# Split prefetch of the p window in the down projection of a Mamba layer with a ternary FFN

## The chip, the cores and the metric

The kernel runs on 8 cores of one Trainium2 chip, one batch row per core. The metric is device time in microseconds of the slowest core, lower is better.

## The reference, cut to what matters

The layer adds a Mamba block and a ternary gated FFN to its input. The part touched by the change is the last matrix product of the FFN, `ternary_matmul(p, W_d)`:

```python
def ternary_matmul(x, w):
    return jnp.matmul(x, jnp.sign(w).T)
xq = activation_quant(rms_norm(x))
g = jax.nn.silu(ternary_matmul(xq, W_g))
u = ternary_matmul(xq, W_u)
p = g * u
return ternary_matmul(p, W_d)
...
xn = _layernorm(x, axis=-1)
x = x + mamba(xn, ...) + ffn(xn, W_g, W_u, W_d)
```

Per core, x is 2048 tokens by 2048 features, p is 2048 tokens by 8192, and `W_d` is 2048 by 8192. So the product is [2048 x 8192] by [8192 x 2048], with weights that are only +1, 0 or -1.

## The kernel before, in words

The program records instructions by hand into one stream for each engine (`streams`), in the order of the Python code. `W` adds a wait on an engine's own counter (`ve`, `sc`, `te`, `gp`), `I` adds an instruction, `LD` adds a load issued by SyncE on a lane (a semaphore `la0` to `la16`), `ST` adds a store issued by GpSimd (`sa0` to `sa7`), and `WT` waits for a load or a store. An engine works its stream strictly in order. All large tiles are views into one SBUF tensor `PA`, so almost every row of the profile names `PA`; the line number tells them apart.

The stages in order of time:

1. Statistics, quantisation and transposes (lines 210 to 334).
2. The input projection, with the casts of the gate and up weights beside it (lines 336 to 439). Its matmuls are line 414.
3. Eight chunks of 256 tokens: convolution, selective scan and output gate on VectorE and ScalarE, with the gate and up products of the FFN on TensorE in between (lines 441 to 742). p goes to the DRAM tensor `psp`, laid out [128, 4 windows, 64, 512].
4. The down projection (lines 744 to 810), the stage that the change touches.
5. The output projection of the Mamba block, and the final sum (lines 812 to 885). Its matmuls are line 862; its window loads (line 851, `ygsp`) are 4 MB each.

Stage 4 runs over `mg` (4 groups of 512 output features). For each group it loads sixteen 1 MB pieces of `wdT` through two staging slots (line 768, lanes 10 and 11), and ScalarE writes their signs as bf16 into `wdb` (line 776), a single buffer of 64 blocks of 512 columns. The load of a piece waits until the Sign two pieces earlier has freed its slot; the first Sign of a group waits for the last matmul of the group before. Then `wdw` runs over 4 windows of 512 tokens. For each, SyncE waits for the last matmul of the window before (`te_p6a_grp`), and loads the whole 8 MB window of p into the single buffer `pwin` (line 786, lane 12). Then `ms` runs over 4 blocks of 128 output features: 64 matmuls of 128x512 accumulate in one PSUM bank (line 794), ScalarE copies the bank to `ostf` (line 801, two slots), and GpSimd stores it to `offn` (line 805). Banks `pb0` to `pb3` rotate as `(ms + wdw) % 4`.

```python
W("sync", "te", te_p6a_grp)
t_pw = LD(lambda e, w=wdw: e.dma_start(
    out=pwin[:], in_=psp[:, w, :, :]), 12)
for ms in range(4):
    bank = (ms + wdw) % 4
    ...
    WT("tensor", t_pw)
    W("tensor", "sc", ev_bank6[bank])
    for k in range(KH):
        I("tensor", ... wdb[:, k, ms * 128:(ms + 1) * 128], pwin[:, k, :] ...)
te_p6a_grp = C["te"]
```

In SyncE's stream the four window loads of a group stand behind the sixteen `wdT` loads of that group, and the `wdT` loads of the next group behind them.

Of the kernel before, what the change touches and what calls it, by code (L numbers as in the profile page):

```python
# [24 lines left out]
KH = H // 128  # L25
# [7 lines left out]
def build_program():  # L33
# [23 lines left out]
    psp = nc.dram_tensor("psp", [128, 4, KH, 512], BF16, kind="Internal").ap()  # L57
# [3 lines left out]
    C = {"ve": 0, "sc": 0, "te": 0, "gp": 0}  # L61
# [5 lines left out]
    with contextlib.ExitStack() as ctx:  # L67
# [4 lines left out]
        def W(eng, sem, val):  # L72
            if val and val > 0:
                streams[eng].append(lambda e, s=sems[sem], v=val: e.wait_ge(s, v))
# [3 lines left out]
        def I(eng, builder, sem=None, amt=1, nodep=False):  # L78
            own = _SELF.get(eng)
            if nodep:  # L80
                own = None
            if own is not None and C[own] > 0 and sem is not None:
                streams[eng].append(
                    lambda e, s=sems[own], v=C[own]: e.wait_ge(s, v))
            if sem is not None:
                C[sem] += amt
                streams[eng].append(
                    lambda e, b=builder, s=sems[sem], a=amt: b(e).then_inc(s, a))
            else:
                streams[eng].append(lambda e, b=builder: b(e))  # L90
            return C[sem] if sem else None

        def LD(builder, lane):
            i = lane
            ld_cnt[i] += 16
            streams["sync"].append(
                lambda e, b=builder, s=ldsem[i]: b(e).then_inc(s, 16))
            return ("L", i, ld_cnt[i])
# [15 lines left out]
        def WT(eng, *toks):  # L114
            for tok in toks:
                if tok is None:
                    continue
                kind, i, v = tok
                s = ldsem[i] if kind == "L" else stsem[i]
                streams[eng].append(lambda e, s=s, v=v: e.wait_ge(s, v))  # L120

        def st_snap():
# [24 lines left out]
        pb = [ctx.enter_context(nc.psum_tensor(f"pb{i}", [128, 512], F32))  # L147
              for i in range(8)]
# [12 lines left out]
        def vb(off_f32, *shape):  # L161
            n = int(np.prod(shape))
            ap = PAb[:, 2 * off_f32: 2 * off_f32 + n]
            if len(shape) == 3:
                ap = ap.rearrange("p (a b c) -> p a b c", b=shape[1], c=shape[2])
            elif len(shape) == 2:
                ap = ap.rearrange("p (a b) -> p a b", b=shape[-1])
            return ap
# [111 lines left out]
        for tt in range(NT):  # L280
# [47 lines left out]
            for h2 in range(2):  # L328
                t_qtt = ST(lambda e, tt=tt, h2=h2: e.dma_start(
                    out=qsp[:, h2 * 8:(h2 + 1) * 8, tt * 128:(tt + 1) * 128],  # L330
                    in_=qtt[:, h2 * 8:(h2 + 1) * 8, :]), 0)
# [59 lines left out]
        for mg in range(16):  # L391
# [14 lines left out]
            for ms in range(4):  # L406
                row = mg * 4 + ms
                xsl = ms % 2
                for wdw in range(4):
                    bank = (ms * 4 + wdw) % 4  # L410
                    W("tensor", "ve", ev_cast)
                    W("tensor", "ve", ev_bank_sc[bank])
                    for k in range(16):
# [3 lines left out]
                            start=(k == 0), stop=(k == 15)), "te")  # L417
# [11 lines left out]
                    out=dst[:, drow, :], in_=xzst[:, xsl, :]), 1 + xsl)  # L429
# [109 lines left out]
        for cI in range(NCH):  # L539
# [6 lines left out]
            if cI == 0:  # L546
# [3 lines left out]
                out=qwin[:, h2 * 8:(h2 + 1) * 8, :],  # L550
                in_=qsp[:, h2 * 8:(h2 + 1) * 8, col0:col0 + TCH]), 7)
# [3 lines left out]
            if cI == 0:  # L555
# [10 lines left out]
                for q4 in range(4):  # L566
                    t_xpre = LD(lambda e, q4=q4: e.dma_start(
                        out=xpre[:, q4 * 8:(q4 + 1) * 8, 3:259],
                        in_=xsp[:, q4 * 8:(q4 + 1) * 8, 0:TCH]), 5)
            else:  # L570
                for q4 in range(4):
                    t_xpre = LD(lambda e, col0=col0, q4=q4: e.dma_start(
                        out=xpre[:, q4 * 8:(q4 + 1) * 8, :],
                        in_=xsp[:, q4 * 8:(q4 + 1) * 8, col0 - 3: col0 + TCH]), 5)
            W("sync", "ve", ev_zread_ve)
            for q4 in range(4):
                t_z = LD(lambda e, col0=col0, q4=q4: e.dma_start(
                    out=zb[:, q4 * 8:(q4 + 1) * 8, :],
# [107 lines left out]
            for dt in range(KDI):  # L686
# [27 lines left out]
                if g == 7:  # L714
# [5 lines left out]
                        in_=yg8[:]), 5)  # L720
# [26 lines left out]
        MARKS["P5"] = {k: len(v) for k, v in streams.items()}  # L747

        wdb = vb(0, KH, 512)
        pwin = vb(16384, KH, 512)  # L750
        wd_big = [vf(32768, 4, 512), vf(34816, 4, 512)]
        wdT_t = wdT.rearrange("(k p) l -> p k l", p=128)
        ostf = vf(36864, 2, 512)
        t_ost2 = [None, None]
        te_p6a_grp = 0
        ev_bank6 = [sc_p3] * 4
        ev_sgn = [0, 0]
        W("tensor", "ve", ve_p3)
        for mg in range(4):
            for q in range(16):  # L760
                sl = q % 2
                if mg == 0 and q == 0:
                    W("sync", "ve", ve_p5)
                    W("sync", "sc", sc_p5)
                    for tok in snap_p3:
                        WT("sync", tok)
                W("sync", "sc", ev_sgn[sl])
                t_wd = LD(lambda e, q=q, mg=mg, sl=sl: e.dma_start(
                    out=wd_big[sl][:],
                    in_=wdT_t[:, q * 4:(q + 1) * 4, mg * 512:(mg + 1) * 512]), 10 + sl)  # L770
                WT("scalar", t_wd)
                if mg == 0 and q == 0:
                    W("scalar", "ve", ve_p5)
                if q == 0:
                    W("scalar", "te", te_p6a_grp)
                ev_sgn[sl] = I("scalar", lambda e, q=q, sl=sl: e.activation(
                    wdb[:, q * 4:(q + 1) * 4, :].rearrange("p a b -> p (a b)"),
                    wd_big[sl][:].rearrange("p a b -> p (a b)"), AF.Sign), "sc")
            sc_wd = C["sc"]
            for wdw in range(4):  # L780
                if mg == 0 and wdw == 0:
                    for tok in snap_p5:
                        WT("sync", tok)
                    W("sync", "ve", ve_p5)
                W("sync", "te", te_p6a_grp)
                t_pw = LD(lambda e, w=wdw: e.dma_start(
                    out=pwin[:], in_=psp[:, w, :, :]), 12)
                for ms in range(4):
                    bank = (ms + wdw) % 4
                    W("tensor", "sc", sc_wd)  # L790
                    WT("tensor", t_pw)
                    W("tensor", "sc", ev_bank6[bank])
                    for k in range(KH):
                        I("tensor", lambda e, k=k, ms=ms, bank=bank: e.matmul(  # L794
                            pb[bank][:], wdb[:, k, ms * 128:(ms + 1) * 128], pwin[:, k, :],
                            start=(k == 0), stop=(k == KH - 1)), "te")
                    te_mm = C["te"]
                    W("scalar", "te", te_mm)
                    osl = (ms + 4 * wdw) % 2
                    WT("scalar", t_ost2[osl])  # L800
                    sc_ost = I("scalar", lambda e, bank=bank, osl=osl: e.activation(
                        ostf[:, osl, :], pb[bank][:], AF.Copy), "sc")
                    ev_bank6[bank] = sc_ost
                    W("gpsimd", "sc", sc_ost)
                    t_ost2[osl] = ST(lambda e, mg=mg, ms=ms, w=wdw, osl=osl: e.dma_start(
                        out=offn[:, mg * 4 + ms, w * 512:(w + 1) * 512], in_=ostf[:, osl, :]), 1 + 3 * osl)
                te_p6a_grp = C["te"]
        snap_p6a = st_snap()
        sc_p6a = C["sc"]
# [161 lines left out]
```

## Time and profile before

| what | us |
|---|---|
| median of 2 runs | 13253.68 (13243.57 to 13263.78) |
| the profiled execution, its own time | 13226.75 |
| its span, slowest core (core 3) | 13225.2 |
| spans of the eight cores | 13171.5 to 13225.2 |
| stage 4, first load of `wdT` to the last matmul, core 3 | 10868.5 to 12405.2 |

Times in the profile are counted from the first instruction of the core. "PE" is TensorE's matmuls and "PEld" its weight loads, "DVE" is VectorE, "ACT" ScalarE, "POOL" GpSimd and "SPq" the loads issued by SyncE. Matmul records overlap each other (each lasts longer than the distance to the next), so the rate of matmuls is read from a run of them, not from the mean of one. PEclk is the clock that TensorE was granted, as a share of its full speed of 2.4 GHz.

### The profile page before, as it was taken

What the parts mean: (1) busy time and instruction counts of PE and PEld (TensorE: products, weight loads), DVE (VectorE), ACT (ScalarE), POOL (GpSimd) and SP (SyncE); (2) the same over time, 40 slices, a digit from 0 to 9 for tenths busy, and PEclk for the clock granted to TensorE, in tenths of its full rate; (3) what the DMA queues carried; (4) which work ended last, traced back from release to release, by engine and by line L of the source; (5) the groups of instructions that cost most, each with busy time, mean ns of one, the idle gap of its engine ahead of it and who ended that gap; (6) DMA issues with size and microseconds to landing.
All of it is one profiled execution on the core that took longest, in us unless ns stands there. A gap on an engine that the chain in (4) does not pass through costs nothing.

```text
span 13225.2 us, 104989 instructions; the slowest of 8 cores (13171.5 to 13225.2 us)
## 1 busy us (share of the span) xinstructions
PE 5051.7 (38%) x28160; PEld 3051.0 (23%) x28160; DVE 7270.3 (55%) x8002; ACT 4306.0 (33%) x7239; POOL 767.6 (6%) x1286
## 2 busy tenths in 40 slices
PE   0116666333223323323313322323323326556666
PEld 0002222122222212212212212212212222222222
DVE  7661111368768768858858858867886870000011
ACT  1221222254344444434434434434435440111000
POOL 0002222100000000000000000000000000000000
PEclk9999888666666656656656666666666668778778
DMA  2106676412212212212212211222221233333354
GB/s 85 33 23 191 194 208 205 143 62 89 88 47 91 91 44 91 90 48 89 89 52 83 91 65 70 91 66 70 89 81 62 84 104 138 148 147 138 147 196 172
DMA packets 607800, 1354.33 MB, mean 102 GB/s; under 512 B 43504, under 2 KB 387696, under 8 KB 533232
## 3 DMA queue, kind: packets, MB, share of 16 engines
q1 hardware_dynamic: 539632, 1154.60, 26.5%
q0 software_dynamic: 67584, 193.02, 4.0%
q8 instruction: 236, 3.87, 0.1%
q14 instruction: 348, 2.85, 0.1%
HBM read 1154.51 MB, written 192.94 MB: 102 GB/s over the span
## 4 chain that ended last, share of the span: by engine, by line
DVE 44%; DMA 18%; PE 13%; ACT 12%; issue 11%; SPq 1%; DVEq 1%; ACTq 0%; POOL 0%; POOLq 0%
DVE PA L692 13%; DVE PA L696 9%; PE pb L794 7%; ACT dA L680 5%; DMA wgusp<-PA 5%; DVE PA L673 4%; PE pb L862 4%; DMA PA<-wuT 3%; DMA PA<-psp 3%; DVE PA L697 2%; DVE PA L300 2%; DMA PA<-ygsp 2%; DVE PA L588 2%; DVE PA L592 2%; DMA PA<-wgT 2%
## 5 line engine op out<-in xcount | busy, mean ns | idle before, releaser
L503 PE MATMUL pb<-PA 128*128 128x256 bf16 x8192 | 1377.3, 340 | 4480.9 <-DVE PA L529 4464.3
L692 DVE TENSOR_TENSOR_SCAN PA<-dA,hcar,PA 128x256 f32<-128x256 f32 x3840 | 2494.6, 726 | 39.3 <-ACT dA L680 14.6
L680 ACT ACTIVATE dA<-PA,a_sb 128x256 f32<-128x256 bf16 x3840 | 1949.4, 508 | 477.0 <-DVE PA L673 134.8
L503 PEld LDWEIGHTS pb<-PA 128*128 128x128 bf16 x8192 | 966.7, 120 | 4812.7 <-issue 4547.0
L877 DVE TENSOR_TENSOR PA<-pb,PA 128x512 f32<-128x512 f32 x64 | 44.3, 692 | 2255.1 <-PE pb L862 2255.1
L680 ACT ACT_TABLE_LOAD x240 | 307.9, 1283 | 2702.3 <-DVE PA L673 2702.3
L794 PE MATMUL pb<-PA 128*128 128x512 bf16 x4096 | 929.1, 391 | 633.9 <-DMA PA<-psp 633.9
L414 PE MATMUL pb<-PA 128*128 128x512 bf16 x4096 | 958.3, 398 | 499.7 <-DVE PA L398 379.4
L696 DVE TENSOR_TENSOR PA<-PA 128x4096 bf16<-128x4096 f32 x256 | 1133.0, 4426 | 27.7 <-DVE PA L692 1.4
L507 PE MATMUL pb<-PA 128*128 128x256 bf16 x8192 | 1098.1, 293 | 0.0
L507 PEld LDWEIGHTS pb<-PA 128*128 128x128 bf16 x8192 | 874.4, 107 | 170.3
L422 DVE CAST PA<-pb 128x512 bf16<-128x512 f32 x256 | 177.1, 692 | 1183.8 <-DMA xsp<-PA 467.3
L363 ACT ACTIVATE PA<-PA 128x512 bf16<-128x512 f32 x512 | 322.2, 629 | 1184.9 <-DMA PA<-wuT 621.0
L536 POOL DMA_DIRECT2D psp<-PA x512 | 276.1, 539 | 7433.1 <-DVE PA L529 7396.0
L794 PEld LDWEIGHTS pb<-PA 128*128 128x128 bf16 x4096 | 409.8, 100 | 1153.0 <-issue 710.0
L414 PEld LDWEIGHTS pb<-PA 128*128 128x128 bf16 x4096 | 413.5, 102 | 1044.2 <-issue 610.9
L529 DVE TENSOR_TENSOR PA<-PA,pb 128x256 bf16<-128x256 bf16 x512 | 215.7, 421 | 784.7 <-DMA psp<-PA 679.2
L862 PE MATMUL pb<-PA 128*128 128x512 bf16 x2048 | 506.4, 415 | 302.9 <-DMA PA<-ygsp 302.9
L673 DVE TENSOR_TENSOR PA<-PA 128x4096 bf16<-128x4096 bf16 x256 | 586.7, 2292 | 27.0 <-DVE PA L671 0.5
L665 DVE TENSOR_TENSOR PA<-PA 128x2048 bf16<-128x2048 bf16 x32 | 73.4, 2293 | 752.7 <-ACT PA L663 752.7
L613 PE MATMUL pb<-PA,wx_bf 128*128 128x256 bf16 x256 | 47.3, 371 | 1100.6 <-DVE PA L607 1100.6
L314 PE MATMUL pb<-identb,PA 128*128 128x128 bf16 x512 | 127.7, 265 | 886.6 <-DVE PA L303 860.6
(101 smaller groups left out, 5314.0 us busy)
## 6 DMA issues: line engine op xcount, KB each, us to landing
PA<-wgusp SPq DMA_DIRECT2D x512, 1024.0 KB, 4.7
PA<-winT SPq DMA_DIRECT2D x32, 2048.0 KB, 21.0
PA<-wgT SPq DMA_DIRECT2D x256, 256.0 KB, 4.3
wgusp<-PA POOLq DMA_DIRECT2D x512, 128.0 KB, 3.9
PA<-wuT SPq DMA_DIRECT2D x256, 256.0 KB, 4.2
PA<-wdT SPq DMA_DIRECT2D x64, 1024.0 KB, 6.2
PA<-ygsp SPq DMA_DIRECT2D x16, 4096.0 KB, 14.0
PA<-xrow SPq DMA_DIRECT2D x32, 1024.0 KB, 4.8
```

What stands on the lines that cost most here:

```text
L300: I("vector", lambda e, c=cbit: e.scalar_tensor_tensor(tq, mk, -c, tq, ALU.mult, ALU.add), "ve")
L363: csc[sl] = I("scalar", lambda e, sl=sl: e.activation(cslot_b[sl][:], cslot_f[sl][:].rearrange("p a b -> p (a b)"), AF.Sign), "sc")
L414: I("tensor", lambda e, k=k, ms=ms, w=wdw, bank=bank: e.matmul(pb[bank][:], wbf[:, k, ms * 128:(ms + 1) * 128], xnT[:, k, w * 512:(w + 1) ...
L503: I("tensor", lambda e, k=k, bank=bank, sl=sl: e.matmul(bank[:, 0:TCH], wgu_sl[sl][:, 0, k, :], qwin[:, k, :], start=(k == 0), stop=(k == ...
L507: I("tensor", lambda e, k=k, bank=bank, sl=sl: e.matmul(bank[:, TCH:2 * TCH], wgu_sl[sl][:, 1, k, :], qwin[:, k, :], start=(k == 0), stop= ...
L536: sl2=sl2: e.dma_start(out=psp[:, w4, ht, coff:coff + TCH], in_=pst2[:]), 6 + sl2)
L673: return I("vector", lambda e: e.tensor_tensor(dbx_b[:], dxdtb[:].unsqueeze(1).broadcast_to([128, DS, TCH]), b_all[:], ALU.mult), "ve")
L680: exp_sc[n] = I("scalar", lambda e, dt=dt, n=n: e.activation(dAs_t[n][:], delta[:, dt, :], AF.Exp, scale=a_sb[:, dt, n:n + 1]), "sc")
L692: I("vector", lambda e, n=n, dt=dt: e.tensor_tensor_scan(hall[:, n, :], dAs_t[n][:], dbx_b[:, n, :], hcar[:, dt, n:n + 1], ALU.mult, ALU.a ...
L696: I("vector", lambda e: e.tensor_tensor(ct[:], hall[:], c_all[:], ALU.mult), "ve")
L794: I("tensor", lambda e, k=k, ms=ms, bank=bank: e.matmul(pb[bank][:], wdb[:, k, ms * 128:(ms + 1) * 128], pwin[:, k, :], start=(k == 0), st ...
L862: I("tensor", lambda e, k=k, ms=ms, bank=bank: e.matmul(pb[bank][:], wob[:, k, ms * 128:(ms + 1) * 128], ygwin[:, k, :], start=(k == 0), s ...
```

## The change

`pwin` is cut into two halves, `pwinH[0]` (k 0 to 31) and `pwinH[1]` (k 32 to 63), each with a lane of its own (12 and 13) and in the same place of `PA` as before. Each window is now worked in two passes: k 0 to 31 for all four `ms`, which opens four banks, then k 32 to 63 for all four, which closes them one by one; only then are they copied out. The first half's buffer is loaded with the next window as soon as the first pass has ended, the second half's as soon as the second has. The two halves of the very first window are loaded ahead of the stage's first `wdT` piece. The window after the last of a group is window 0 again, so the prefetch runs on across groups.

```diff
-        pwin = vb(16384, KH, 512)
+        pwinH = [vb(16384, 32, 512), vb(24576, 32, 512)]
...
+        W("sync", "te", te_p3c)
+        for tok in snap_p3:
+            WT("sync", tok)
+        pw_tok = [LD(lambda e, h=h: e.dma_start(
+            out=pwinH[h][:], in_=psp[:, 0, h * 32:(h + 1) * 32, :]), 12 + h)
+            for h in range(2)]
...
-                W("sync", "te", te_p6a_grp)
-                t_pw = LD(lambda e, w=wdw: e.dma_start(
-                    out=pwin[:], in_=psp[:, w, :, :]), 12)
+                widx = mg * 4 + wdw
+                nw = (widx + 1) % 4
+                W("tensor", "sc", sc_wd)
+                WT("tensor", pw_tok[0])
                 for ms in range(4):
                     bank = (ms + wdw) % 4
-                    W("tensor", "sc", sc_wd)
-                    WT("tensor", t_pw)
                     W("tensor", "sc", ev_bank6[bank])
-                    for k in range(KH):
+                    for k in range(32):
                         I("tensor", lambda e, k=k, ms=ms, bank=bank: e.matmul(
-                            pb[bank][:], wdb[:, k, ms * 128:(ms + 1) * 128], pwin[:, k, :],
-                            start=(k == 0), stop=(k == KH - 1)), "te")
+                            pb[bank][:], wdb[:, k, ms * 128:(ms + 1) * 128],
+                            pwinH[0][:, k, :],
+                            start=(k == 0), stop=False), "te")
+                pw_te[0] = C["te"]
+                if widx + 1 < 16:
+                    W("sync", "te", pw_te[0])
+                    pw_tok[0] = LD(lambda e, nw=nw: e.dma_start(
+                        out=pwinH[0][:], in_=psp[:, nw, 0:32, :]), 12)
+                WT("tensor", pw_tok[1])
+                for ms in range(4):
+                    bank = (ms + wdw) % 4
+                    for k in range(32):
+                        I("tensor", lambda e, k=k, ms=ms, bank=bank: e.matmul(
+                            pb[bank][:], wdb[:, 32 + k, ms * 128:(ms + 1) * 128],
+                            pwinH[1][:, k, :],
+                            start=False, stop=(k == 31)), "te")
                     te_mm = C["te"]
...
+                pw_te[1] = C["te"]
+                if widx + 1 < 16:
+                    W("sync", "te", pw_te[1])
+                    pw_tok[1] = LD(lambda e, nw=nw: e.dma_start(
+                        out=pwinH[1][:], in_=psp[:, nw, 32:64, :]), 13)
                 te_p6a_grp = C["te"]
```

SyncE's stream before, from the start of stage 4 into its second group (`te`, `sc`, `ve` are the engines' counters, `sa0` to `sa7` the stores):

```order
L768 DMA PA<-wdT 128x4x512 [waits ve,sc,sa0,sa1,sa2,sa3,sa4,sa5,sa6,sa7]
L768 DMA PA<-wdT 128x4x512
L768 DMA PA<-wdT 128x4x512 [waits sc] x14
L786 DMA PA<-psp 128x32768 [waits sa0,sa1,sa2,sa3,sa4,sa5,sa6,sa7,ve]
L786 DMA PA<-psp 128x32768 [waits te] x3
L768 DMA PA<-wdT 128x4x512 [waits sc] x16
L786 DMA PA<-psp 128x32768 [waits te] x4
```

SyncE's stream of the changed kernel, from the start of stage 4:

```order
L765 DMA PA<-psp 128x16384 [waits ve,sc,te,sa0,sa1,sa2,sa3,sa4,sa5,sa6,sa7]
L765 DMA PA<-psp 128x16384
L778 DMA PA<-wdT 128x4x512 [waits ve,sc,sa0,sa1,sa2,sa3,sa4,sa5,sa6,sa7]
L778 DMA PA<-wdT 128x4x512
L778 DMA PA<-wdT 128x4x512 [waits sc] x14
L806 DMA PA<-psp 128x16384 [waits te]
L829 DMA PA<-psp 128x16384 [waits te]
```

The window's two halves moved from behind the sixteen pieces to ahead of them. The same stream of the changed kernel, where the first group ends and the second begins:

```order
L806 DMA PA<-psp 128x16384 [waits te]
L829 DMA PA<-psp 128x16384 [waits te]
L778 DMA PA<-wdT 128x4x512 [waits sc] x16
L806 DMA PA<-psp 128x16384 [waits te]
L829 DMA PA<-psp 128x16384 [waits te]
```

Before, nothing that waits for TensorE's last matmul of the group stood ahead of the next group's `wdT` pieces; now the load of line 829 does, and they are issued behind it.

TensorE's stream before, at the end of the first window and the start of the second (`pb` is the bank, `la12` the lane of the window load):

```order
L794 MATMUL pb3<-PA 128x512 [waits sc,la12]
L794 MATMUL pb3<-PA 128x512 x63
L794 MATMUL pb1<-PA 128x512 [waits sc,la12]
L794 MATMUL pb1<-PA 128x512 x63
L794 MATMUL pb2<-PA 128x512 [waits sc,la12]
L794 MATMUL pb2<-PA 128x512 x63
```

The same place in the changed kernel, from the last bank of the first pass of window 1 to the first pass of window 2:

```order
L799 MATMUL pb3<-PA 128x512 [waits sc]
L799 MATMUL pb3<-PA 128x512 x31
L812 MATMUL pb0<-PA 128x512 [waits la13]
L812 MATMUL pb0<-PA 128x512 x31
L812 MATMUL pb1<-PA 128x512 x32
L812 MATMUL pb2<-PA 128x512 x32
L812 MATMUL pb3<-PA 128x512 x32
L799 MATMUL pb1<-PA 128x512 [waits sc,la12]
L799 MATMUL pb1<-PA 128x512 x31
L799 MATMUL pb2<-PA 128x512 [waits sc]
L799 MATMUL pb2<-PA 128x512 x31
```

A bank is now opened once, left, and closed 128 matmuls later, and the four banks are closed at a distance of 32 matmuls instead of 64.

## Rows read from the trace of the kernel before

**Rows 1.** Part 5 of the page: the matmuls of stage 4.

```profile
L794 PE MATMUL pb<-PA 128*128 128x512 bf16 x4096 | 929.1, 391 | 633.9 <-DMA PA<-psp 633.9
```

**Rows 2.** Timeline of TensorE in stage 4 (start, us, what, [idle before <-releaser]), 8 of 16 windows.

```profile
10955.31 57.90 PE L794 MATMUL pb<-PA 128*128 128x512 bf16 x256 [113.14 <-DMA PA<-psp]
11036.57 58.22 PE L794 MATMUL pb<-PA 128*128 128x512 bf16 x256 [23.36 <-DMA PA<-psp]
...
11200.90 57.98 PE L794 MATMUL pb<-PA 128*128 128x512 bf16 x256 [24.20 <-DMA PA<-psp]
11340.33 58.23 PE L794 MATMUL pb<-PA 128*128 128x512 bf16 x256 [81.46 <-DMA PA<-psp]
11421.42 56.96 PE L794 MATMUL pb<-PA 128*128 128x512 bf16 x256 [22.85 <-DMA PA<-psp]
...
11720.76 57.47 PE L794 MATMUL pb<-PA 128*128 128x512 bf16 x256 [81.86 <-DMA PA<-psp]
...
12100.24 57.17 PE L794 MATMUL pb<-PA 128*128 128x512 bf16 x256 [80.15 <-DMA PA<-psp]
...
12341.00 64.21 PE L794 MATMUL pb<-PA 128*128 128x512 bf16 x256 [22.81 <-DMA PA<-psp]
```

**Rows 3.** Timeline of TensorE in stage 2: one run of 64 matmuls.

```profile
1522.77 13.97 PE L414 MATMUL pb<-PA 128*128 128x512 bf16 x64 [1.89 <-DVE PA L422]
```

**Rows 4.** Timeline, SyncE's loads and the outer Signs, first and second group.

```profile
10868.53 61.70 SPq L768 DMA_DIRECT2D PA<-wdT  x16
10874.88 1.91 ACT L776 ACTIVATE PA<-PA 128x2048 bf16<-128x2048 f32 x1 [14.15 <-DMA PA<-wdT]
...
10935.86 1.91 ACT L776 ACTIVATE PA<-PA 128x2048 bf16<-128x2048 f32 x1 [1.62 <-DMA PA<-wdT]
...
11177.18 138.71 SPq L768 DMA_DIRECT2D PA<-wdT  x16
...
11259.77 3.91 ACT L776 ACTIVATE PA<-PA 128x2048 bf16<-128x2048 f32 x2
...
11315.99 82.99 SPq L786 DMA_DIRECT2D PA<-psp  x2
11320.88 1.91 ACT L776 ACTIVATE PA<-PA 128x2048 bf16<-128x2048 f32 x1 [2.81 <-DMA PA<-wdT]
```

**Rows 5.** Chain of waits: window loads of 8 MB (`psp`) and of 4 MB (`ygsp`).

```profile
11398.64 22.53 DMA PA<-psp
...
12528.49 13.90 DMA PA<-ygsp
...
12681.93 12.96 DMA PA<-ygsp
...
12831.40 18.84 DMA PA<-ygsp
```

**Rows 6.** DMA issues: KB each, median us from issue to landing.

```profile
PA<-wdT SPq DMA_DIRECT2D x64, 1024.0 KB, 6.2
PA<-ygsp SPq DMA_DIRECT2D x16, 4096.0 KB, 14.0
```

**Rows 7.** The stores of line 805, by line.

```profile
DMA to landing us min/median/max: 2.3/2.3/17.8
```

**Rows 8.** Windows, core 3: busy (x) of PE PEld DVE ACT POOL, PEclk, DMA share, GB/s.

```profile
11440.00:11460.00 20.00, 20.00 (x94) 9.11 (x93) 0.00 (x0) 0.60 (x1) 0.54 (x1) 1.00 0.04 15
...
12380.00:12400.00 20.00, 20.00 (x78) 8.27 (x76) 0.00 (x0) 0.60 (x1) 0.54 (x1) 0.81 0.04 14
11640.00:11720.00 80.00, 0.00 (x0) 0.00 (x0) 0.00 (x0) 30.34 (x16) 0.54 (x1) 0.52 0.84 292
11398.00:11421.00 23.00, 0.57 (x3) 0.07 (x1) 0.00 (x0) 0.60 (x1) 0.54 (x1) 0.56 0.90 376
...
1780.00:1800.00 20.00, 20.00 (x94) 9.07 (x93) 2.77 (x4) 5.04 (x8) 5.33 (x10) 1.00 0.73 208
```

**Rows 9.** Windows in stage 5, core 2, then core 0: same columns.

```profile
12411.00:12440.00 29.00, 28.60 (x104) 11.73 (x105) 4.16 (x6) 0.00 (x0) 1.62 (x3) 0.77 0.20 56
...
12420.00:12440.00 20.00, 20.00 (x91) 8.93 (x90) 2.77 (x4) 0.00 (x0) 1.08 (x2) 0.97 0.30 72
```

More of the change, by code:

```diff
@@ L755, in build_program @@
         te_p6a_grp = 0
+        te_p3c = C["te"]
         ev_bank6 = [sc_p3] * 4
@@ L758, in build_program @@
         W("tensor", "ve", ve_p3)
+        W("sync", "ve", ve_p5)
+        W("sync", "sc", sc_p5)
+        W("sync", "te", te_p3c)
[4 more added lines that the diff above has]
+            for h in range(2)]
+        pw_te = [0, 0]
         for mg in range(4):
@@ L780, in build_program @@
             for wdw in range(4):
[L781 to L784, printed above, removed]
-                W("sync", "te", te_p6a_grp)
-                t_pw = LD(lambda e, w=wdw: e.dma_start(
-                    out=pwin[:], in_=psp[:, w, :, :]), 12)
+                widx = mg * 4 + wdw
+                nw = (widx + 1) % 4
+                W("tensor", "sc", sc_wd)
+                WT("tensor", pw_tok[0])
                 for ms in range(4):
                     bank = (ms + wdw) % 4
-                    W("tensor", "sc", sc_wd)
-                    WT("tensor", t_pw)
                     W("tensor", "sc", ev_bank6[bank])
-                    for k in range(KH):
+                    for k in range(32):
                         I("tensor", lambda e, k=k, ms=ms, bank=bank: e.matmul(
-                            pb[bank][:], wdb[:, k, ms * 128:(ms + 1) * 128], pwin[:, k, :],
-                            start=(k == 0), stop=(k == KH - 1)), "te")
+                            pb[bank][:], wdb[:, k, ms * 128:(ms + 1) * 128],
[14 more added lines that the diff above has]
+                            start=False, stop=(k == 31)), "te")
                     te_mm = C["te"]
```

## The prediction

> **What bounds the kernel now.** I read the page's groups first. The matmuls of the down projection (line 794) are busy for 929.1 us, and ahead of them TensorE sat idle for 633.9 us, all of it until a load of `psp` landed [rows 1]. The timeline of TensorE shows how these are spread: sixteen windows of 256 matmuls, some 57 to 58 us each. Ahead of the first window of a group the gap is 113.14, 81.46, 81.86 and 80.15 us; ahead of the twelve others it is about 23 us [rows 2]. The twelve sum to 633.9 - (113.14 + 81.46 + 81.86 + 80.15) = 277.3 us. The reader is to see strict alternation: the load of an 8 MB window takes 22.53 us in the chain of waits [rows 5], TensorE does nothing meanwhile, and while TensorE computes, the DMA engines stand at a share of 0.04 [rows 8]. Nothing else in this stage ends last: the bank copies and the stores run beside the matmuls. The long gaps have another content: sixteen Signs of `wdT` pieces and then the window load [rows 4].
>
> **The twelve inner gaps.** After the change a half window (4 MB) is loaded while the other half is computed. How long is a pass of 128 matmuls? From a run of 64 in 13.97 us [rows 3], of which one record is about 0.38 us, the distance is (13.97 - 0.38) / 63 = 0.2157 us; a pass is 27.6 us and a window 256 x 0.2157 + 0.2 = 55.4 us. How long is a 4 MB load? `ygsp` windows have that size: 12.96 and 13.90 us where they run alone, 18.84 at the longest where they share [rows 5], 14.0 in the median [rows 6]. So 13 us lie under 27.6 us, and even 19 would. The gaps go: 277.3 us.
>
> **The clock's start.** In a gap the granted clock falls to 0.52 or 0.56, near the lower of its two levels (1.2 of 2.4 GHz), and within a window it is 1.00 [rows 8]. So each window starts slow. The sixteen windows took 929.1 us [rows 1] where sixteen at full clock take 16 x 55.4 = 886.4. Of the 42.7 us over, 6.3 belong to the last window, which took 64.21 instead of some 57.9 [rows 2]. That leaves 36.4 / 16 = 2.3 us a window. Twelve windows will follow without a gap: 12 x 2.3 = 27 us.
>
> **The three later group starts.** Before, the first two `wdT` pieces of a group were issued 82 us before its first Sign (11177.18), the first Sign ran at 11259.77, the sixteenth at 11320.88, and the window load was issued at 11315.99 [rows 4]; the gap was 81.46 us [rows 2]. Now SyncE must first wait for the group's last matmul and issue the second half of the window, and the pieces stand behind it. One half takes 13 us, and a 1 MB piece behind it comes about 2.8 us later (8 MB in 22.53 us [rows 5]). So the first Sign starts some 16 us after the last matmul. The pace afterwards stays: 61.1 us from the first to the sixteenth Sign (11320.88 - 11259.77; 60.98 in the first group [rows 4]) and 1.9 for the last one. Both halves are in SBUF by then, so matmuls start at 16 + 61.1 + 1.9 = 79 us. Gain: 2 to 2.5 us each, 7 together. It is small because what the half window saves at the end it costs at the start: the prefetch of the pieces is given up.
>
> **The stage's start.** Before: 10868.53 (first issue) to 10955.31 (first matmul), 86.8 us [rows 2, 4]. Now 22.5 us for both halves, about 2.8 for the first piece, then 61 and 1.9: 88.2, plus a little issue time, so 2 us lost. With the line above it makes +5. The bounds of the two: if pieces and half share the engines without delay, the group starts gain up to 13 us each (the half simply vanishes), +39; if the pieces come as late as with the 18.84 us load [rows 5], -6 us each, -18. I take +5, since a load of 4 MB takes 13 to 14 us in two of the three rows and in the median.
>
> **Waits that the change adds.** The halves' waits stand ahead of a pass, on TensorE; behind them is the whole stage, and they are met as worked out above. The four banks are now closed 6.9 us apart instead of 13.8. ScalarE's copy waits for the store of two copies earlier, which is 13.8 us back; stores land in 2.3 us, at the longest in 17.8 [rows 7]. One store of 17.8 us would hold a copy by some 4 us, and TensorE wants a closed bank again no earlier than 14 us after its closing (the bank order in front of the next window is turned by one). So I cost it at 0; with the cover gone it would be 4 us a window. The matmuls' number and size do not change. Sync's other loads are not in this stage.
>
> **Sum.** 277.3 + 27 + 7 - 2 = 309 us. The profiled execution took 13226.75, so it becomes 12918. It stands 26.9 under the median of the runs, 13253.68, which becomes 12945. That is 2.3% less. A measurement of this kernel can tell about 2% from no change, 265 us, which leaves 44 us of room, so the size of what is given back decides how it counts.
>
> **Rival 1: the denser work brings a lower clock.** In core 3's last window the rate fell from 94 matmuls in 20 us at a clock of 1.00 to 78 at 0.81 [rows 8], and in stage 5 core 2 stood at 0.77 while core 0 stood at 0.97 in the same microseconds [rows 9]. So there is a state at about 0.81, which came while TensorE was busy on all cores. After the change TensorE has runs of 4 x 55.4 = 221 us instead of 58. At 0.81 a window costs 55.4 / 0.81 - 55.4 = 13.0 us more. If all sixteen are so, 208 less the 6.3 already paid: 202 given back, and the time is 12945 + 202 = 13147. With eight windows, 98 given back: 13043. From 44 / 13.0 = 3.4 windows more than now, the result is within 2%. Against it: fifteen of core 3's sixteen windows took 57 to 58 us, with all eight cores in this stage at the same time, so 58 us of dense matmuls do not bring it. For it: no row shows a run longer than that, and the slowest core counts, of eight. The Trainium skill ("TensorE: Matmul & The Clock Gate", Part 1: The HAM clock gate) warns that once three cores of a die run dense matmuls a current limiter takes the whole die to 13/16 of the full clock and holds it there; it adds that this depends on the data. The level agrees with the 0.81 of the rows, the reach does not: here single cores are slowed and most windows never are. Taken literally the rule would have each window already at 13/16, which they are not, and the change would then give nothing back; as a risk that grows with density it is this rival.
>
> **Rival 2: the prefetch is only half covered.** If the eight cores, whose loads now overlap matmuls, crowd each other or the stores, a half may take longer than its pass. Each us beyond 27.6 costs 24 us over the 24 inner halves. The 44 us of room are gone at 29.4 us for a half, and at 32 us the time is 12945 + 106 = 13051. For it: 18.84 us where a 4 MB load shared the engines [rows 5]. Against: the eight cores already load 8 MB in 22.5 us at 376 GB/s at nearly the same time [rows 8], and the mean need falls to 4 MB in 27.6 us, 152 GB/s.
>
> **Rival 3, the slower side: DMA writes into SBUF slow the matmuls.** Before, matmuls of this stage ran with the DMA engines at 0.04 [rows 8]; now a load lies beside half of their time, and writes the same tensor that TensorE reads. The place is the 24 inner passes, 665 us. It decides for slower than before only if these passes take 309 / 665 = 46% longer, 40 us each instead of 27.6; at 60% longer the time is 12945 + 399 = 13344. Against: in stage 2, 94 matmuls ran in 20 us at a DMA share of 0.73 and 208 GB/s [rows 8], the same rate as without any.
>
> **Chances.** The forecast 60%, the lower clock in enough windows to matter 32%, the half covered prefetch 5%, the slower matmuls 3%. The range begins at 12895 (the last window's 6 us and up to 39 at the group starts gained) and must leave out no more than 2 in 10: it ends at 13110, between eight windows at the lower clock (13043) and all sixteen (13147). Faster by over 2% (under 12989) holds in the forecast and a little of rival 1: 0.62. Within 2%: 0.35. Slower by over 2%: 0.03.
>
> **What would show it.** TensorE's timeline in the down projection should show four runs of about 224 us without a gap, then gaps of some 79 us; idle ahead of these matmuls waiting for `psp` should be under 10 us in the inner windows. A first Sign 16 us after a group's last matmul, and a half landing in 13 to 19 us, are the other two steps. The granted clock within a run should be 1.00; a clock near 0.81, or under 90 matmuls in 20 us, is rival 1. Gaps between passes are rival 2. A full clock with under 90 matmuls in 20 us is rival 3. The forecast is wrong if core spans fall by less than 265 us.

## The result, and the profile after

The changed kernel took 12969.84 us in the median of 11 runs (12897.29 to 13157.75); the kernel before took 13256.27 us (10 runs) beside it. The ratio is 0.9767, with a 95% interval of 0.9725 to 0.981. Run again later on another chip the ratio was 0.9723 (0.9635 to 0.9811). Both ratios are taken over the executions in which no die lagged behind at a lower clock (9 of these 11, later 2 of 6), so the first isn't the quotient of the medians, which is 0.9784. The forecast was 12945 us, a ratio of 0.9767 to the 13253.68 us known then: faster, by a little more than the 2% that a measurement can tell. That the kernel got faster is clear; that it did so by more than 2% is likely and not settled, since both intervals reach a little over 0.98. That forecast and measurement agree to the fourth digit is luck.

The page of the changed kernel shows the matmuls of the down projection, in two groups for the two passes, and the groups view shows their idle time:

```profile
L799 PE MATMUL pb<-PA 128*128 128x512 bf16 x2007 | 451.6, 385 | 345.8 <-ACT PA L786 343.6 <-issue 0.2
L812 PE MATMUL pb<-PA 128*128 128x512 bf16 x2007 | 442.3, 379 | 2.2
```

They answer to [rows 1]. No idle time is put down to a load of `psp` any more; what is left is four waits for the last Sign (line 786), 343.6 us in all. (Some 2% of the matmul records are missing from this trace, hence 2007 of 2048.)

Timeline of TensorE, changed kernel, core 2, the first group, then the first pass of the other three; the columns are those of [rows 2]:

```profile
10997.08 30.18 PE L799 MATMUL pb<-PA 128*128 128x512 bf16 x125 [116.04 <-ACT PA L786]
11027.09 27.79 PE L812 MATMUL pb<-PA 128*128 128x512 bf16 x125
11054.72 27.79 PE L799 MATMUL pb<-PA 128*128 128x512 bf16 x126
11082.34 27.79 PE L812 MATMUL pb<-PA 128*128 128x512 bf16 x125
...
11192.85 27.79 PE L812 MATMUL pb<-PA 128*128 128x512 bf16 x125
11297.28 30.45 PE L799 MATMUL pb<-PA 128*128 128x512 bf16 x125 [76.65 <-ACT PA L786]
...
11596.24 1.01 PE L799 MATMUL pb<-PA 128*128 128x512 bf16 x2 [75.12 <-ACT PA L786]
...
11894.85 30.33 PE L799 MATMUL pb<-PA 128*128 128x512 bf16 x126 [75.76 <-ACT PA L786]
...
12090.78 27.79 PE L812 MATMUL pb<-PA 128*128 128x512 bf16 x126
```

The reader is to see eight passes that follow each other every 27.63 us with nothing in between, then one long gap. Only the first pass of a group is longer, by 2.4 to 2.7 us: that is the slow start of the clock, which each of the sixteen windows paid before. Two windows of the view, with the columns of [rows 8], show the clock and the DMA in a gap and in a run:

```profile
11240.00:11290.00 50.00, 0.00 (x0) 0.00 (x0) 0.00 (x0) 24.95 (x14) 0.00 (x0) 0.50 0.83 271
11360.00:11380.00 20.00, 19.95 (x93) 9.04 (x93) 0.00 (x0) 0.00 (x0) 0.00 (x0) 1.00 0.35 145
```

In the gap the clock stands at 0.50, the lower of its levels (1.2 GHz), in the run at 1.00 (2.4 GHz). The loads of the first half, by line, landed in:

```profile
DMA to landing us min/median/max: 12.5/13.3/14.9
```

The loads of the second half (line 829) take 12.8 to 14.5 us. One half takes half of the pass that covers it.

### The profile page after: what moved, and what is told of

Same layout as the page of the kernel before. It is cut to its first block, busy times and chain, and to the rows that moved or that the text cites. A ratio compares the mean times of both kernels' runs of the same rounds, so it can differ in the third digit from the quotient of the medians.

```text
span 12919.3 us, 104737 instructions; the slowest of 8 cores (12870.3 to 12919.3 us)
## 1 busy us (share of the span) xinstructions
PE 4983.0 (39%) x27955; PEld 3029.2 (23%) x28160; DVE 7270.3 (56%) x8002; ACT 4305.9 (33%) x7239; POOL 760.1 (6%) x1286
## 4 chain that ended last, share of the span: by engine, by line
DVE 46%; DMA 16%; PE 13%; issue 12%; ACT 12%; SPq 1%; DVEq 1%; ACTq 0%; POOL 0%; POOLq 0%
DVE PA L692 14%; DVE PA L696 9%; ACT dA L680 5%; DMA wgusp<-PA 5%; DVE PA L673 5%; DMA PA<-wuT 3%; PE pb L799 3%; PE pb L812 3%; PE pb L886 3%; DVE PA L697 2%; DVE PA L300 2%; DMA PA<-ygsp 2%; DMA PA<-wdT 2%; DVE PA L588 2%; DVE PA L592 2%
## 5 line engine op out<-in xcount | busy, mean ns | idle before, releaser
L503 PEld LDWEIGHTS pb<-PA 128*128 128x128 bf16 x8192 | 958.7, 119 | 4821.8 <-issue 4551.4
L414 PE MATMUL pb<-PA 128*128 128x512 bf16 x4014 | 968.9, 403 | 529.1 <-DVE PA L398 401.3
L507 PEld LDWEIGHTS pb<-PA 128*128 128x128 bf16 x8192 | 871.2, 106 | 172.2
L414 PEld LDWEIGHTS pb<-PA 128*128 128x128 bf16 x4096 | 417.6, 103 | 1080.2 <-issue 655.8
L886 PE MATMUL pb<-PA 128*128 128x512 bf16 x2007 | 472.9, 397 | 317.2 <-DMA PA<-ygsp 314.6
L799 PE MATMUL pb<-PA 128*128 128x512 bf16 x2007 | 451.6, 385 | 345.8 <-ACT PA L786 343.6
L812 PE MATMUL pb<-PA 128*128 128x512 bf16 x2007 | 442.3, 379 | 2.2
```

The lines of the kernel that those rows point to most:

```text
L414: I("tensor", lambda e, k=k, ms=ms, w=wdw, bank=bank: e.matmul(pb[bank][:], wbf[:, k, ms * 128:(ms + 1) * 128], xnT[:, k, w * 512:(w + 1) ...
L503: I("tensor", lambda e, k=k, bank=bank, sl=sl: e.matmul(bank[:, 0:TCH], wgu_sl[sl][:, 0, k, :], qwin[:, k, :], start=(k == 0), stop=(k == ...
L507: I("tensor", lambda e, k=k, bank=bank, sl=sl: e.matmul(bank[:, TCH:2 * TCH], wgu_sl[sl][:, 1, k, :], qwin[:, k, :], start=(k == 0), stop= ...
L799: I("tensor", lambda e, k=k, ms=ms, bank=bank: e.matmul(pb[bank][:], wdb[:, k, ms * 128:(ms + 1) * 128], pwinH[0][:, k, :], start=(k == 0) ...
L812: I("tensor", lambda e, k=k, ms=ms, bank=bank: e.matmul(pb[bank][:], wdb[:, 32 + k, ms * 128:(ms + 1) * 128], pwinH[1][:, k, :], start=Fal ...
L886: I("tensor", lambda e, k=k, ms=ms, bank=bank: e.matmul(pb[bank][:], wob[:, k, ms * 128:(ms + 1) * 128], ygwin[:, k, :], start=(k == 0), s ...
```

## The experiments

Six of the eight runs change one thing in the changed kernel or build on it; two repeat kernels. To set the kernels side by side without the cores that were granted a lower clock (more on them below), "undisturbed span" here means the median span of those cores, over all executions, whose mean granted clock was within 0.003 of the highest of that kernel. It is 13189.5 us for the kernel before (122 of 248 core spans) and 12882.9 us for the changed one (86 of 144): 307 us less. e1 to e4 ran on one chip, e5 and e6 on a second, e7 and e8 on a third; the kernel before, run beside them, had an undisturbed span of 13197, 13170 and 13194 us there, so a comparison across chips can be off by some 25 us.

**e1: no overlap.**

```diff
-                if widx + 1 < 16:
-                    W("sync", "te", pw_te[0])
-                    pw_tok[0] = LD(... pwinH[0] ...)
...
                     W("sync", "te", pw_te[1])
+                    pw_tok[0] = LD(... pwinH[0] ...)
                     pw_tok[1] = LD(... pwinH[1] ...)
```

> The changed kernel with one edit: the first half's next load is no longer issued after the first pass but, like the second half's, after the window's last matmul. Two passes, two halves and the bank order stay. Theory (the gain is the load time that now lies under matmuls): each of the 12 inner gaps comes back as the time of one 4 MB load, 13 to 14 us, plus 2.3 us of slow clock, about 190 us; the second half lands under the first pass. At the three group starts a second 4 MB load stands ahead of the wdT pieces, 9 us each, 28 us. Together +218 us over the changed kernel, near 0.995 of the kernel before. Rival (the two-pass order of the banks, not the overlap, brought the gain): stays within 20 us of the changed kernel.

Measured: 13221.32 us, ratio to the kernel before 0.9949 (0.9918 to 0.998), undisturbed span 13098 us, 215 over the changed kernel where 218 were expected. Timeline of TensorE, core 4:

```profile
11054.19 30.64 PE L799 MATMUL pb<-PA 128*128 128x512 bf16 x128 [13.33 <-DMA PA<-psp]
11084.66 27.79 PE L808 MATMUL pb<-PA 128*128 128x512 bf16 x128
11125.68 30.73 PE L799 MATMUL pb<-PA 128*128 128x512 bf16 x128 [13.23 <-DMA PA<-psp]
11156.25 27.79 PE L808 MATMUL pb<-PA 128*128 128x512 bf16 x128
11272.58 30.67 PE L799 MATMUL pb<-PA 128*128 128x512 bf16 x128 [88.54 <-ACT PA L786]
```

The gap is back, with the slow start behind it, and it is 13.3 us rather than 23, because the second half lands under the first pass. Splitting the load brings 10 us a window, and issuing it a pass earlier the rest. The order of the banks brings nothing by itself: e1 is 92 us under the kernel before, and twelve gaps that are 10 us shorter, less three group gaps that are some 8 us longer (86.82 to 90.06 us), leave nothing for it.

**e2: each half loaded twice.**

```diff
                     pw_tok[0] = LD(... pwinH[0] ...)
+                    if wdw < 3:
+                        WT("sync", pw_tok[0])
+                        pw_tok[0] = LD(... pwinH[0] ...)
```

and the same for the second half.

> The changed kernel, but within a group each half is loaded, awaited, and loaded a second time, so that twice the bytes lie beside the inner passes: two loads of 13 us are 26 us, under a pass of 27.6 us. Theory (a half is covered with a factor of two to spare, and DMA writes beside the matmuls do not slow them): within 20 us of the changed kernel, matmuls at 0.2157 us, inner gaps under 1 us. Rival 2 of the prediction (crowding makes a half take longer than its pass when traffic is higher): gaps of several us in each of 21 inner passes, +50 us or more. Rival 3 (DMA writes into SBUF slow the matmuls): passes longer than 27.8 us at a full clock.

Measured: 13034.85 us, ratio 0.9801 (0.9728 to 0.9875), undisturbed span 12942 us, 59 over the changed kernel. That is a miss for my "within 20 us", and on the side of rival 2, for which I had written 50 us or more. Timeline of TensorE and the landing of line 806's loads, core 2:

```profile
11089.56 30.04 PE L799 MATMUL pb<-PA 128*128 128x512 bf16 x128 [6.31 <-DMA PA<-psp]
11119.43 27.79 PE L816 MATMUL pb<-PA 128*128 128x512 bf16 x128
11149.99 27.79 PE L799 MATMUL pb<-PA 128*128 128x512 bf16 x128 [2.77 <-DMA PA<-psp]
11178.75 27.79 PE L816 MATMUL pb<-PA 128*128 128x512 bf16 x128 [0.97 <-DMA PA<-psp]
...
DMA to landing us min/median/max: 13.3/14.9/16.7
```

With twice the bytes (DMA share 0.79 from 10993 to 11217 us, 278 GB/s) a load of the first half takes 14.9 us instead of 13.3, and its repetition 15.4; for the second half it is 16.2 and 14.5 instead of 14.0. Two take 30.3 or 30.7 us, over the 27.6 us of a pass; the inner gaps sum to 45 us, and several restart at a slow clock (29.2 to 30.0 us a pass). Crowding (rival 2) is real, but at most some 2 us a load in size: the cover has a factor of 1.8, not endless. Rival 3 is refuted: passes that follow without a long gap last 27.79 us with twice the DMA writes beside them, to the hundredth what they last in the changed kernel.

**e3: the second half behind the pieces.**

```diff
             sc_wd = C["sc"]
+            if mg > 0:
+                W("sync", "te", pw_te[1])
+                pw_tok[1] = LD(... pwinH[1], psp[:, 0, 32:64, :] ...)
...
-                if widx + 1 < 16:
+                if widx + 1 < 16 and wdw < 3:
                     W("sync", "te", pw_te[1])
```

> The changed kernel with one load moved: at the three group changes the second half of the window is issued behind the sixteen wdT pieces instead of ahead of them, so that the first two pieces are prefetched again. Theory (the group's start is the first piece's wait for that half plus the chain of Signs): the first Sign follows the last matmul by under 1 us instead of 16, the group gaps fall from 75 to 77 us to 64 us (0.7 + 61.1 + 1.9), and the second half, issued some 56 us after the last matmul, lands before the second pass wants it. 3 x 12 = 36 us less than the changed kernel. Rival (the pace of pieces is set by DMA throughput and the half only moves): no gain, or a new wait ahead of the second pass.

Measured: 12994.74 us, ratio 0.9759 (0.9666 to 0.9851), undisturbed span 12847 us, 36 under the changed kernel where 36 were expected; the ratios themselves are too close to tell the two apart, so the gain is read from the timeline. Timeline around a group change, core 0:

```profile
11169.66 0.60 ACT L824 ACTIVATE PA<-pb 128x512 f32<-128x512 f32 x1 [6.31 <-PE pb L816]
11170.35 3.91 ACT L786 ACTIVATE PA<-PA 128x2048 bf16<-128x2048 f32 x2
...
11223.76 0.46 SPq L792 DMA_DIRECT2D PA<-psp  x1
...
11230.91 4.40 PE L803 MATMUL pb<-PA 128*128 128x512 bf16 x13 [61.45 <-ACT PA L786]
```

The first Sign follows the last bank copy at once, the gap is 61.45 us, and the half issued at 11223.76 is not waited for: the pass behind it starts at 11259.97 without idle time. The other two group gaps of this core are 60.77 and 61.65 us.

**e4: Signs early.** The sixteen pieces of a group are no longer worked in a block. On ScalarE two Signs of the next group stand ahead of each bank copy of the last window's second pass, and eight behind them; TensorE's first pass waits for the eighth Sign, its second for the sixteenth.

```diff
+                if last and nxt:
+                    W("scalar", "te", pw_te[0])
                 for ms in range(4):
+                    if last and nxt:
+                        step(mg + 1, 2 * ms)
+                        step(mg + 1, 2 * ms + 1)
...
+                if last and nxt:
+                    W("scalar", "te", pw_te[1])
+                    for q in range(8, 16):
+                        step(mg + 1, q)
```

(`step` is one Sign and the load of a later piece; the loads of the two halves stand behind the loads of pieces 5 and 9.)

> A version that may beat both: the Signs of the next group's first eight pieces run beside the second pass of the last window (their half of the weights is no longer read then), the other eight beside the first pass of the next group; the window's halves are issued among the pieces, and the stage starts likewise with a first pass after eight pieces. Theory (the group gap is a chain of sixteen Signs at 3.9 to 4.1 us each that nothing but the single weight buffer forbids to hide): the gap ahead of a group falls to about 8 us, another of about 12 us stands ahead of its second pass, so 3 x 56 = 168 us less than the changed kernel, and some 25 us at the stage's start: near 12780 us. Rival (the chip is out of DMA throughput there: 12 MB in a pass of 27.6 us is over 400 GB/s, above the 376 GB/s seen): the gaps add up to 40 us or more a group, and the gain is under 110 us.

Measured: 12901.45 us, ratio 0.9674 (0.9582 to 0.9766), undisturbed span 12723 us, 160 under the changed kernel where some 190 were expected, and the median is 121 us over the 12780 of the expectation; 24 of the 32 core spans were at the lower clock. Timeline of TensorE at a group change, core 2:

```profile
11140.89 27.79 PE L836 MATMUL pb<-PA 128*128 128x512 bf16 x128
11180.70 30.32 PE L823 MATMUL pb<-PA 128*128 128x512 bf16 x128 [12.02 <-ACT PA L782]
11226.45 29.63 PE L836 MATMUL pb<-PA 128*128 128x512 bf16 x128 [15.44 <-ACT PA L782]
```

The 76 us have become 12 and 15: 27 to 30 us at the three group changes instead of the 20 expected, below the 40 of the rival.

**e5: a third staging slot.**

```diff
-        wd_big = [vf(32768, 4, 512), vf(34816, 4, 512)]
+        wd_big = [vf(32768, 4, 512), vf(34816, 4, 512), vf(37888, 4, 512)]
```

> The early-Signs version with a third staging slot for wdT pieces. In it the gaps ahead of a group were 10 to 13 us and ahead of its second pass 15 to 17 us, all until a Sign. Theory A (the gaps are the ping-pong of two slots: a piece's 6 us to land plus its Sign, twice): with three slots the eight pieces come faster, both gaps fall by half or more, 3 x 14 = 42 us and some 15 us at the start less than with two. Theory B (DMA throughput: pieces and halves, 12 MB in a pass, already take all that the engines give): less than 15 us change in all.

Measured: 12831.79 us, ratio 0.9662 (0.9555 to 0.977), undisturbed span 12667 us, 55 under e4, but on another chip, where the kernel before was 27 us shorter too. Core 1 of this trace beside core 2 of e4's, both undisturbed in this stage, shows 37 (start of the stage 10, three group changes 27), between the 57 of theory A and the 15 of theory B. Its timeline and its windows:

```profile
11138.28 30.22 PE L823 MATMUL pb<-PA 128*128 128x512 bf16 x128 [9.23 <-ACT PA L782]
11177.67 29.31 PE L836 MATMUL pb<-PA 128*128 128x512 bf16 x128 [9.18 <-ACT PA L782]
```

```profile
11118.00:11146.00 28.00, 18.77 (x77) 7.88 (x75) 0.00 (x0) 10.79 (x8) 1.08 (x2) 0.82 0.99 363
```

Between the two theories: the ping-pong was part of it. Around the start of the group the DMA engines are now at 0.99 and 363 GB/s, where e4 had 0.92 and 321 GB/s in the same 28 us (11160 to 11188 on its core 2). That throughput is what is left is likely; no run shows it.

**e6: the output projection too.** `ygwin` becomes two buffers of 4 MB, and the load of window i + 1 is issued at the head of window i.

```diff
-        ygwin = vb(8192, KDI, 512)
+        ygwin2 = [vb(8192, KDI, 512), vb(28672, KDI, 512)]
...
+                for yn in ([0, 1] if yi == 0 else [yi + 1]):
+                    if yn < 16:
+                        W("sync", "te", yg_te[yn % 2])
+                        yg_tok[yn % 2] = LD(... ygwin2[yn % 2], ygsp[:, yn % 4, :, :] ...)
```

> The version with three slots, and the output projection's window of ygsp (4 MB) double-buffered in free SBUF, each load issued one window ahead. The same mechanism in the next stage: 12 inner gaps of 13 to 14 us (some 17) plus 2.3 us of slow clock each, 190 us, and the window load at each group start, 13 to 17 us, about 50 us. Together 230 us less than the three-slot version if a matmul stage gains what its uncovered loads took. Rival (in this stage TensorE waits next for the final sum on VectorE or for the xcol and offn loads, which share the DMA engines): under 120 us, with waits for VectorE ahead of the matmuls.

Measured: 12690.14 us, ratio 0.9556 (0.9456 to 0.9657), undisturbed span 12493 us, 174 under e5 (same chip) where 230 were expected. Timeline of TensorE in that stage, core 5:

```profile
11897.59 112.91 PE L926 MATMUL pb<-PA 128*128 128x512 bf16 x512 [39.54 <-DMA PA<-ygsp]
12043.37 113.40 PE L926 MATMUL pb<-PA 128*128 128x512 bf16 x512 [32.86 <-ACT PA L902]
```

The twelve inner gaps are gone (512 matmuls in one run). The gaps at the group changes are not: 32.86, 33.74 and 37.36 us against 35.13, 32.02 and 31.80 in e5. In e5 (core 1) the window load had been the last to land, at 12097.80, and the fourth cast of a `woT` piece (there line 900) had ended 8.7 us earlier. So in that gap at most 9 us could be gained, not the 13 to 17 I had counted. In e6 the gap ends with the fourth cast (line 902), and the casts themselves come later: the first `woT` piece is issued 4.4 us ahead of the group's last matmul (12006.14 against 12010.50) where it was 11.0 us in e5, and its cast starts 8.5 us behind that matmul where it was 2.0. On cores 0 and 1, both at the lower clock in e6, these gaps did fall, from 31.7 to 35.1 us in e5 to 24.4 to 25.8. That is most of the 50 us I had counted too much. Why the pieces are issued later was not tested.

**e7 and e8: the lower clock.** The changed kernel and the kernel of e6, unchanged, in more runs beside the kernel before.

> The changed kernel as it is, beside the kernel before on the same chip, to count cores at the lower clock (mean granted clock more than 0.006 below the highest of the kernel). Rival 1 (denser matmuls bring the lower clock): a clearly larger share of such cores than in the kernel before, and a slowest core that lies further above the undisturbed cores. Theory (the lower clock comes to pairs of cores in either kernel and is not the change's): shares alike within the scatter, about 4 in 10, undisturbed cores 310 to 320 us faster, ratio 0.976.

> The densest version (early Signs, three slots, output projection double-buffered) once more, for the same count. In four runs 22 of 32 core spans were at the lower clock. If density brings it: again over 6 in 10 and the slowest core over 150 us above the undisturbed ones. If that was chance: about 4 in 10, as before. Ratio to the kernel before about 0.955.

Measured: e7 13125.52 us, ratio 0.9723 (0.9635 to 0.9811), undisturbed span 308 us under the kernel before where 310 to 320 were expected; e8 12683.65 us, ratio 0.95 (0.9451 to 0.9548). Cores at the lower clock on that chip: 52 of 88 core spans in the kernel before, 24 of 48 in the changed kernel, 28 of 48 in e8, and the slowest core lay on average 182, 207 and 197 us above the undisturbed ones. What that clock does is seen in e1, whose matmuls are not dense. Windows of core 1, then of core 4 of the same execution, and the timeline of core 1:

```profile
11795.00:11825.00 30.00, 30.00 (x116) 12.40 (x114) 0.00 (x0) 1.79 (x3) 1.62 (x3) 0.81 0.07 26
```

```profile
11795.00:11825.00 30.00, 30.00 (x140) 13.58 (x139) 0.00 (x0) 1.19 (x2) 1.08 (x2) 1.00 0.03 11
```

```profile
11716.94 27.79 PE L808 MATMUL pb<-PA 128*128 128x512 bf16 x128
11758.28 34.15 PE L799 MATMUL pb<-PA 128*128 128x512 bf16 x128 [13.55 <-DMA PA<-psp]
11792.26 33.78 PE L808 MATMUL pb<-PA 128*128 128x512 bf16 x128
```

At 0.81 a pass takes 33.78 us instead of 27.79. It comes over a core within a stage and goes again. Over all executions it was 118 of 248 core spans of the kernel before and 50 of 144 of the changed one, and the slowest core lay 143 and 140 us above the undisturbed ones, so the change did not bring it. For the densest versions it stays open: e4, e5 and e6 had 24, 24 and 22 of 32, more than the kernel before beside them (44 of 104, and 22 of 56), but e8 had no more than its neighbour. The count itself leans that way, since a kernel with a larger share of its time in matmuls loses more of its mean clock for the same spell.

## Why the prediction was right

The stage's own balance, from core 3 before and core 2 after, first load to last matmul: 1536.7 us before, 1211.0 after, 325.7 less. That pair flatters the change. Over all eight cores of the same two traces the stage took 1519.6 to 1542.1 us before and 1209.3 to 1223.5 after, 316.8 less in the mean. By the steps of the prediction:

- The twelve inner gaps, 277.3 us: gone whole; the mean of the eight cores was 281.5. A half lands in 12.5 to 14.9 us under a pass of 27.63; 13 and 27.6 were the working's numbers. e1 brings a gap of 13.3 us back in each place, and with it and the longer group starts 215 us.
- The clock's start, 27 us, and 6.3 us of the last window that the forecast left in: the stage's time outside its gaps fell from 929.1 to 894.0 us on the pair, 35.1 where 33.3 would follow. In the mean of the eight cores it fell by 28.5, of which core 3's slow last window is 1. That window was simply not slowed after the change.
- The three group starts, 7 us: 15.9 on the pair (gaps of 76.65, 75.12 and 75.76 where 79 was worked out), but 7.6 in the mean of the eight cores (80.3 us a gap before, 77.8 after, single ones from 75.1 to 82.0). The pace of the pieces stays, as the working said: 58.9 us in the mean from the first to the sixteenth Sign before, 58.7 after. The 61.1 that the working took is that of a slow core, the 56.8 of core 2 (11238.22 to 11294.98) that of a fast one. The first Sign came 17.6 us after the last matmul there, 16.9 in the mean, where 16 was said. The three gaps of core 0 show how wide the spread is:

```profile
11238.93 29.62 PE L799 MATMUL pb<-PA 128*128 128x512 bf16 x128 [78.27 <-ACT PA L786]
11543.98 30.68 PE L799 MATMUL pb<-PA 128*128 128x512 bf16 x128 [82.04 <-ACT PA L786]
11848.94 30.10 PE L799 MATMUL pb<-PA 128*128 128x512 bf16 x128 [80.90 <-ACT PA L786]
```

  That the half ahead of the pieces takes back what the prefetch gives was right: e3 moves it behind them, and the first Sign follows at once.
- The stage's start, 2 us lost: 2.7 lost on the pair (89.5 us instead of 86.8), 0.7 in the mean.
- The waits added, 0: the bank copies waited for nothing but matmuls, and no pass waited for a bank.

The sum of 309 us stands against 316.8 in the stage and 307 between the undisturbed spans. That it meets the second to 2 us is partly luck: in the two traces the stages ahead of the change, which it doesn't touch, took 20 us longer after it in the mean (the stage began at 10862 us before and 10882 after, 10873 in e7), and those behind it 8 us less. The median came out 25 us above the forecast. The medians are those of the slowest core, and they fell by 286 us only. The slowest core lay 67 us above the undisturbed span in the median before and 87 after, which is a matter of how many of some ten executions had a spell at the lower clock: seven of the 18 executions of the changed kernel had no such core, and their slowest still lay 13 to 97 us above.

Of the rivals, the first named a real thing and a wrong cause. The level of about 0.81 exists, costs 6.0 us a pass (13.0 a window were worked out, 12.0 measured), and made single executions as slow as 13157.75 us, 13179.7 in e7; but it takes the kernel before at least as often. The rule of the Trainium skill ("TensorE: Matmul & The Clock Gate", Part 1: The HAM clock gate), 13/16 of the clock for a whole die under dense all-core matmuls, has the level right. In the trace of e7 cores 4 and 5 stood at 0.81 in this stage while cores 6 and 7 of the same die had 1.00, and in the trace of the changed kernel all eight cores ran their 223 us of dense matmuls without it. The second would need loads of over 27.6 us, nearly twice what e2 made them. The third is refuted by e2. The chance of 0.35 for "within 2%" can't be judged by one case, but it wasn't idle: the interval, 0.9725 to 0.981, just reaches over 0.98.

## What to carry to other kernels

Where a single large buffer forces load and matmuls to alternate and there is no room for a second one, cut the contraction in two: each half's buffer is refilled while the other is used, at the price of keeping all accumulators of the window open. The gain is the idle time plus the clock's slow start behind each gap. Then look at what the new order puts behind the new wait: the loads queued behind a prefetch that waits for the last matmul lost their own prefetch, and putting the half behind them (e3), and then the next group's weights beside matmuls (e4, e5), brought another 36 to 216 us between undisturbed spans. Read such a balance from all cores: two cores picked from two traces made a gain of 7.6 us look like 15.9. Work hidden just below the longest wait is paid when that wait goes, as with the casts of `woT` in e6.

## What was new about the hardware

- In a stage the lower clock comes to pairs of neighbouring cores; over an execution it is a matter of the die. Windows of e7, core 4, then core 6 of the same die:

```profile
11050.00:11100.00 50.00, 49.65 (x188) 20.71 (x190) 0.00 (x0) 2.39 (x4) 2.16 (x4) 0.81 0.53 189
1350.00:1650.00 300.00, 181.98 (x753) 78.18 (x768) 50.79 (x56) 65.46 (x104) 75.09 (x117) 0.81 0.69 201
```

```profile
11050.00:11100.00 50.00, 50.00 (x233) 22.70 (x232) 0.00 (x0) 1.79 (x3) 1.62 (x3) 1.00 0.47 168
1350.00:1650.00 300.00, 207.12 (x768) 84.23 (x768) 47.19 (x52) 64.21 (x102) 72.79 (x115) 0.72 0.68 199
```

  In stage 4 cores 4 and 5 are slowed, 6 and 7 not. From 1350 to 1650 us it is the other way round: a stretch with pauses in it, in which the undisturbed core 0 has 0.80 too. The two cores that the prediction's rows show at the lower clock, 3 and 2, are such a pair as well. In e7 all four cores of the die end with a low mean clock: 0.696, 0.695, 0.700 and 0.700, where the other die has 0.720. So it is in most cases: in 31 executions of the kernel before, with two dies each, 29 dies had all four cores at the lower clock, one had two, and 32 none; in the 18 of the changed kernel 11 dies had all four, three had one to three, and 22 none. Only the span tells whether it hurts: cores 6 and 7 took 12860.5 and 12870.7 us, no more than undisturbed ones.
- A 4 MB load slows only from 13.3 or 14.0 to 14.5 to 16.2 us when all cores load twice the bytes, and matmuls do not feel the writes into the tensor they read: 27.79 us a pass either way.
